# Delta rule stage: order of PE, ACT, DVE and POOL work around the block inverse changed

## The reference

```python
mixed = lax.conv_general_dilated(mixed, conv_w, (1,), [(3, 0)], ...)   # q, k, v: depthwise, 4 taps
g = -jnp.exp(A_log) * jax.nn.softplus(a + dt_bias)
beta = jax.nn.sigmoid(b)
q = _l2norm(q) * DK ** (-0.5)
k = _l2norm(k)
def step(Sstate, xs):
    q_t, k_t, v_t, g_t, b_t = xs
    Sstate = Sstate * jnp.exp(g_t)[..., None, None]
    kv = jnp.einsum('bhk,bhkv->bhv', k_t, Sstate)
    delta = (v_t - kv) * b_t[..., None]
    Sstate = Sstate + k_t[..., :, None] * delta[..., None, :]
    o_t = jnp.einsum('bhk,bhkv->bhv', q_t, Sstate)
    return (Sstate, o_t)
...
o = o * lax.rsqrt(var + EPS) * norm_weight * jax.nn.sigmoid(z)
return o.reshape(Bsz, Sl, VDIM) @ w_out.T
```

## Time and profile before

| | |
|---|---|
| median of 3 runs | 4793.93 us |
| the profiled execution | 4783.35 us, its span 4781.6 us |
| mean granted TensorE clock over the span | 0.881 |
| PE busy | 4103.1 us, 86% of the span |
| DVE busy | 2333.8 us, 49% |
| ACT busy | 1674.0 us, 35% |
| POOL busy | 1300.2 us, 27% |

### The profile page before, as it was taken

The page is one execution under the profiler, slowest core; times in us unless marked ns, Lnnn a source line. Parts: engine busy times, 40 slices in busy tenths (PEclk is TensorE's granted clock), DMA queues, the critical chain, the costliest instruction groups (busy, mean ns, idle before and its releaser), DMA issues. The chain is left out here.

```text
span 4781.6 us, 104546 instructions
## 1 busy us (share of the span) xinstructions
PE 4103.1 (86%) x45120; PEld 2471.8 (52%) x45120; DVE 2333.8 (49%) x4105; ACT 1674.0 (35%) x2632; POOL 1300.2 (27%) x1755
## 2 busy tenths in 40 slices
PE   7789759999965867778899779999999999999869
PEld 3333645555542733445645546655555665556546
DVE  5942244444453233342132256666666666666541
ACT  2057222112120102323111145555555555655432
POOL 2000110000015051220000045555554555555412
PEclk9689759999986985888899879998999999989879
DMA  1000000000020520000100000000000000000000
GB/s 46 1 1 2 28 25 1 10 10 1 10 95 27 172 78 17 0 0 23 54 0 0 5 10 8 9 9 9 9 9 8 10 8 8 8 8 8 6 14 18
DMA packets 37963, 91.85 MB, mean 19 GB/s; under 512 B 6992, under 2 KB 27251, under 8 KB 33998
## 3 DMA queue, kind: packets, MB, share of 16 engines
q1 hardware_dynamic: 27150, 69.45, 4.3%
q0 software_dynamic: 6144, 11.62, 0.8%
q10 hardware_dynamic: 4224, 4.19, 0.3%
HBM read 69.96 MB, written 20.45 MB: 19 GB/s over the span
## 5 line engine op out<-in xcount | busy, mean ns | idle before, releaser
L2498 PE MATMUL ps<-h_normT,h_w 128*128 128x512 f32 (+1 forms) x1008 | 446.0, 549 | 69.8 <-DVE h_xx L3086 62.7
L3020 DVE SCALAR_TENSOR_TENSOR h_cv<-h_raw,h_cw,h_cv 128x1023 f32<-128x1023 f32 (+2 forms) x288 | 385.4, 1339 | 19.8 <-ACT h_cv L2847 18.8
L3164 DVE SCALAR_TENSOR_TENSOR h_st<-h_st,d_gcs,ps 128x64 f32<-128x64 f32 x448 | 122.7, 274 | 402.6 <-PE ps L2795 402.4
L2395 POOL TENSOR_TENSOR h_gm<-h_gm,h_tmp 128x15 f32<-128x15 f32 (+7 forms) x480 | 268.7, 560 | 37.6
L2846 ACT ACTIVATE h_raw<-ps 128x512 f32<-128x512 f32 x192 | 114.1, 594 | 460.0 <-PE ps L2498 459.2
L2498 PEld LDWEIGHTS ps<-h_normT,h_w 128*128 128x128 f32 x1008 | 173.0, 199 | 175.1 <-issue 157.6
L837 PE MATMUL ps<-a_probT,a_v 128*128 128x512 f32 x512 | 227.8, 604 | 0.9 <-DVE a_probT L975 0.9
L1960 PE MATMUL ps<-h_normT,e_wgu 128*128 128x512 f32 (+1 forms) x448 | 203.8, 598 | 3.3 <-DMA e_wd<-in_e_wd 2.7
L2394 POOL TENSOR_TENSOR h_tmp<-h_gm 128x15 f32<-128x15 f32 (+7 forms) x480 | 185.1, 386 | 64.4 <-DVE h_gm L3073 29.3
L1124 POOL MEMSET r_zero<- 128x2048 f32 x1 | 1.8, 1804 | 727.2 <-POOLq L54 727.2
L2795 PEld LDWEIGHTS ps<-h_st,h_mT 64*64 64x64 f32 x1792 | 91.7, 135 | 199.9 <-issue 194.8
(11 more groups left out here) (537 smaller groups left out, 9513.9 us busy)
## 6 DMA issues: line engine op xcount, KB each, us to landing
m_wgu<-in_m_wgu SPq DMA_DIRECT2D x8, 1408.0 KB
h_w<-in_d_w SPq DMA_DIRECT2D x48, 128.0 KB
m_wd<-in_m_wd SPq DMA_DIRECT2D x8, 704.0 KB
m_rows_in<-r_zero SPq DMA_DIRECT2D x4, 1024.0 KB
e_xe<-m_rows_in SPq DMA_DIRECT2D x8, 512.0 KB
m_rows_out<-e_y ACTq DMA_DIRECT2D x8, 512.0 KB
e_wgu<-in_e_wgu SPq DMA_DIRECT2D x1, 3520.0 KB
a_t_raw<-in_t_w SPq DMA_DIRECT2D x4, 768.0 KB
```

Source lines behind the costliest of these rows:

```text
L2395: c.link(pool.tensor_tensor(target, target, part, ALU.subtract))
L2498: last = pe.matmul(ps[:, PROJ[m], lo:hi], w[:, kind, k, :], hT[:, k, b * S + tb * BANK + lo:b * S + tb * BANK + hi], start=(k == 0), stop= ...
L3020: dve.scalar_tensor_tensor(out=d, in0=raw[:, kind, 0:S - back], scalar=tap(pr, kind, TAPS3 - 1 - back), in1=d, op0=ALU.mult, op1=ALU.add). ...
```

## The change

On PE the second key products and the decay sums up to each token go ahead of the second value product. In `states`, the third output product goes from c = 10 to c = 9, and from the first bank of A3 to B3 + 1; the inverse then starts at c = 10; the quarters of projections 4 and 5 are spread over c = 10 to 13, two of projection 4 standing alone at c = 11; the two halves of the last output product stand behind `inverse_below` and `inverse_above`, at c = 14 and 15. On POOL the gating goes first in the step. On ACT both output copies go first, the output squares behind and between the key squares and decays; it compacts two quarters instead of three, ahead of the second value parts. DVE compacts the third quarter, does the transposes and the gathering ahead of the query sums, and has its convolutions, residual sums and copies of the inverse at other q.

```diff
@@ heads3
-        POUT = (B3 + 1, B3 + 1, A3, A3)
+        POUT = (B3 + 1, B3 + 1, B3 + 1, A3)
@@ gpsimd: sided(f)
                 pool.wait_ge(sub, SUBS * (f[0] + 1))
+                if f[0]:
+                    pool.wait_ge(wk, 2 * f[0])
@@ gpsimd: step
+                if t:
+                    gated(t)
                 if f:
                     scaled(f)
                 if t:
                     squares(t)
                 if f:
                     last_quarter(f, t)
-                if t:
-                    gated(t)
-                if f:
                     solve(f)
                     sided(f)
@@ tensor: key_side
                     key_products(f, 0)
+                if f:
+                    hold(k_ev, 3 * f[0] + 3)
+                    key_products(f, 1)
+                    pe.wait_ge(at_d, 2 * f[0] + 1)
+                    decay_upto(f)
                 if t:
                     hold(sqo_d, 2 * n)
                 values_and_keys(1)
-                if f:
-                    hold(k_ev, 3 * f[0] + 3)
-                    key_products(f, 1)
                 key_sums(0)
                 key_sums(1)
-                if f:
-                    pe.wait_ge(at_d, 2 * f[0] + 1)
-                    decay_upto(f)
@@ tensor: states, beside(c)
-                    if c == 9 and f:
+                    if c == 9 and t:
+                        pe.wait_ge(xa, 4 * n + 2)
+                        project_out(t, 2)
+                    if c == 10 and f:
                         if p:
-                            pe.wait_ge(xa, 4 * n + 2) if t else pe.wait_ge(ev, 6 * p[0] + 2)
+                            pe.wait_ge(xa, 4 * n + 3) if t else pe.wait_ge(ev, 6 * p[0] + 2)
                         hold(zv, 2 * n + 2)
-                        inverse_y(f, (lambda k: project(p, 4, k)) if p else None)
-                    if c == 10 and t:
-                        pe.wait_ge(v_ev, f[0] + 1) if f else pe.wait_ge(lnd, 2 * t[0] + 2)
-                        project_out(t, 2)
-                    if c == 11 and f:
+                        inverse_y(f, (lambda k: project(p, 4, k) if k < 2 else None) if p else None)
+                    if c == 11 and p:
+                        for k in (2, 3):
+                            project(p, 4, k)
+                    if c == 12 and f:
                         hold(v_ev, f[0] + 1)
-                        hold(ev, 6 * p[0] + 5) if p else hold(xa, 4 * n + 2)
-                        inverse_z(f, (lambda k: project(p, 5, k)) if p else None)
-                    if c == 12:
-                        if t:
-                            pe.wait_ge(xa, 4 * n + 3)
-                        if f:
-                            inverse_zt(f, (lambda k: out_part(t, 3, 0) if k == 0 else None) if t else None)
-                        elif t:
-                            out_part(t, 3, 0)
-                    if c == 13:
+                        hold(ev, 6 * p[0] + 5) if p else hold(xa, 4 * n + 3)
+                        inverse_z(f, (lambda k: project(p, 5, k) if k < 3 else None) if p else None)
+                    if c == 13 and f:
+                        inverse_zt(f, (lambda k: project(p, 5, 3) if k == 0 else None) if p else None)
+                    if c == 14:
                         if f:
                             inverse_below(f)
                         if t:
+                            pe.wait_ge(v_ev, f[0] + 1) if f else pe.wait_ge(lnd, 2 * t[0] + 2)
+                            out_part(t, 3, 0)
+                    if c == 15:
+                        if f:
+                            inverse_above(f)
+                        if t:
                             out_part(t, 3, 1)
-                    if c == 14 and f:
-                        inverse_above(f)
@@ scalar: step
                 if t:
-                    outputs(t, 0)
+                    outputs(t)
                 if f:
-                    key_squares(f)
+                    key_squares(f, (0,))
                 if t:
-                    outputs(t, 1)
+                    output_squares(t, 0)
                 if f:
+                    key_squares(f, (1,))
                     decays(f)
+                if t:
+                    output_squares(t, 1)
                 parts(0)
+                if f:
+                    compacted(f)
                 parts(1)
...
-                    if f and g == 1:
-                        compacted(f)
@@ scalar: outputs
+            def outputs(t):
+                if t[0]:
+                    act.wait_ge(y_p, 4 * t[0])
+                for a in range(2):
+                    act.wait_ge(o_p, NC3 * t[0] + NC3)
+                    act.activation(chunks(o[:], a), outs(a), ACT.Copy).then_inc(o_d, 1)
+            def output_squares(t, a):
+                act.wait_ge(o_p, NC3 * t[0] + NC3)
+                act.activation(chunks(sqo, a), outs(a), ACT.Square).then_inc(sqo_d, 1)
@@ vector
+            def third_quarter(f):
+                dve.wait_ge(nt_d, 2 * f[0] + 2)
+                dve.tensor_copy(y[quarter(2), :, :], nT[quarter(2), :, side(2)]).then_inc(nc2_d, 1)
@@ vector: step
                     decayed(f, 0)
                     decayed_pairs(f, 0)
-                    convolve(f, 6)
                     decayed(f, 1)
                     decayed_pairs(f, 1)
+                    third_quarter(f)
+                    diagonals(f)
+                    gather(f)
                 for g in range(2):
...
-                if f:
-                    diagonals(f)
-                    gather(f)
...
-                    if f and q in (1, 2):
-                        convolve(f, q + 6)
+                    if f and q in (1, 2, 3):
+                        convolve(f, q + 5)
...
-                    if t and q == 6:
-                        add(t, 0)
-                    if t and q == 8:
-                        add(t, 1)
+                    if t and q in (6, 8, 10):
+                        add(t, (q - 6) // 2)
...
-                    if f and q == 10:
+                    if f and q == 11:
                         masked(f)
-                    if t and q == 11:
-                        add(t, 2)
-                    if f and q in (12, 13):
-                        refined(f, q - 12)
+                    if f and q in (13, 14):
+                        refined(f, q - 13)
...
-                    if p and q in (3, 5, 6, 9, 10, 12):
-                        convolve(p, (3, 5, 6, 9, 10, 12).index(q))
+                    if p and q in (5, 6, 7, 10, 11, 12):
+                        convolve(p, (5, 6, 7, 10, 11, 12).index(q))
```

More of the change, by code:

```diff
@@ L2262, in heads3 @@
                  "sqvr", "bepd", "kev", "vev", "seg", "decd", "dbd", "egp", "egx", "qed", "qsqd", "kk", "ntd", "atd",
-                 "ncd", "nc3d", "xtd", "nqd", "ndd", "sub", "xmd", "xdd", "nx", "yd", "y4d", "xy", "xd", "tt", "xtx", "uwp", "wd", "ud", "wk", "mtd", "ptd",
+                 "ncd", "nc2d", "nc3d", "xtd", "nqd", "ndd", "sub", "xmd", "xdd", "nx", "yd", "y4d", "xy", "xd", "tt", "xtx", "uwp", "wd", "ud", "wk", "mtd", "ptd",
                  "sp", "sd", "loc", "op", "od", "sqod", "sqa", "msp", "lnd", "rsd", "rz", "ond", "yp", "xa")
@@ L2266, in heads3 @@
          sqv_r, bep_d, k_ev, v_ev, seg, dec_d, db_d, eg_p, egx, qe_d, qsq_d, kk, nt_d, at_d,
-         nc_d, nc3_d, xt_d, nq_d, nd_d, sub, xm_d, xd_d, nx, y_d, y4_d, xy, x_d, tt, xtx, uw_p, w_d, u_d, wk, mt_d, pt_d,
+         nc_d, nc2_d, nc3_d, xt_d, nq_d, nd_d, sub, xm_d, xd_d, nx, y_d, y4_d, xy, x_d, tt, xtx, uw_p, w_d, u_d, wk, mt_d, pt_d,
          s_p, s_d, loc, o_p, o_d, sqo_d, sqa, ms_p, lnd, rs_d, rz, on_d, y_p, xa) = (ph.sem(n) for n in names)
@@ L2817, in end @@
                 for k in range(4):
-                    if k in (1, 3):
+                    if k in (1, 2):
                         pe.wait_ge(xa, 4 * n + 4 + k)
-                    if k == 2:
+                    if k == 3:
                         pe.wait_ge(lnd, 2 * n + 2)
@@ L2852, in gate_logits, with key_squares @@
                 act.activation(zs[:, b, half(tb)], ps[:, GATE[tb], :], ACT.Sigmoid).then_inc(zv, 1)
-            def key_squares(f):
+            def key_squares(f, some=range(2)):
                 n = f[0]
-                for a in range(2):
+                for a in some:
                     act.wait_ge(k_ev, 3 * n + 1) if a else act.wait_ge(trk, n + 1)
@@ L2892, in compacted @@
                 act.wait_ge(nt_d, 2 * n + 2)
-                for r in range(3):
+                for r in range(2):
                     act.activation(y[quarter(r), :, :], nT[quarter(r), :, side(r)], ACT.Copy).then_inc(nc_d, 1)
@@ L2988, in step @@
                     inverse_pieces(f)
-            def outputs(t, a):
-                n = t[0]
-                chunks = lambda v, a: v.rearrange("p (j a n) -> p a j n", a=2, n=CH3)[:, a]
-                act.wait_ge(o_p, NC3 * n + NC3)
-                src = ps[:, C3 + a, :].rearrange("p (j n) -> p j n", n=CH3)
```

(17 more changed lines are left out.)

## The result

The changed kernel takes 4932.24 us, the median of 4 runs (4904.42 to 4944.69), against 4793.53 (4789.97 to 4810.0) for the kernel before: ratio 1.0279, 95% interval 1.0252 to 1.0307. It is 2.8% slower. The forecast was 4790 with a range up to 4850: no change was expected, and the time lies 82 us above the range.

What follows compares the result with a forecast made beforehand. The prediction took PE, 86% busy, as the bound, with waits and low clock at the inverse's head and tail. Queues +1.1 and clock -1.2 gave -0.1 per unit, x29 = -3 us: 4790 us, range 4715 to 4850.

Steps and rivals of the forecast that it cites:

- POOL: POOL's substitution before the block inverse: 2.8 us earlier against PE, so POOL leaves the path.
- Head: Head of the block inverse: new stalls of 1.05 (state) and 1.5 us (residual sum) on DVE; net +0.45 per unit.
- Middle: Before chunk 12: PE waits for ACT to copy the fifth projection's bank, +0.9 us per unit.
- Tail: Last small products of the inverse: the 1.09 us wait for DVE's 32-row copy goes, -1.1 per unit.
- Key side: Key products and sums: waits for scaled keys 0.4, decayed pairs 0.1, ACT's copies 0.55; +1.05 per unit, 0.2 hidden.
- Clock: PE's granted clock: -1.5 at the tail, +0.3 at the head, net -1.2 us per unit; about 0.94 over the stage.
- POOL and DVE beside each other: Convolution beside POOL's substitution: each costs the other 0.5 to 0.7 us; taken as hidden, else some +5 us in all.
- B: Rival, chance 0.28: the bank handover puts DVE's queue on PE's path at chunk 10; +1.6 per unit, 4840 us.
- A: Rival, chance 0.23: the clock holds at the tail of the inverse; -1.5 per unit, 4750 us.
- C: Rival, chance 0.11: handovers hide, both PE waits and most low clock go; -3.6 per unit, 4690 us.

Runs made afterwards that it cites:

- e2: The kernel before with only the changed chunk loop and the wait it needs; POOL, ACT and key side in the old order: 4865.87 us, ratio 1.0145.
- e4: The changed kernel with the first three of p's convolutions one state update earlier, at q = 4, 5, 6: 4858.78 us, ratio 1.0122.
- e3: The changed kernel with the second value product again ahead of the second key products, and ACT's two compacted quarters behind its second value parts: 4877.97 us.
- e10: The changed kernel with the third output product back in bank A3, at c = 11, its sum at q = 12; inverse still from c = 10: 4813.57 us.
- e9: The changed kernel with the old key side of the second value product, convolutions at q = 4, 5, 6, 10, 11, 12 and values at q = 11: 4737.72 us.

## Why the prediction was wrong

Per unit it had +1.1 at full clock and -1.2 from the clock; measured are +4.05 and +0.6. The miss is 4.7 us per unit, 2.9 in the queues and 1.8 in the clock. Two steps failed: the head, by its size, and the clock, which had nothing for the stall before chunk 12.

*POOL*: right. It leaves the path, with 7.2 us between its first sided product and the transposes.

*Head*: this step failed by its size. The mechanism, the place and the last two stalls were right (0.88 and 1.53 against 1.05 and 1.5). It began the count at the convolution of q = 7 and took 1.2 for it, with PE and DVE in step until then. They were not: the convolution at q = 5 takes 2.06 and that at q = 7 1.87, and PE waits at the chunks before too. State waits are 2.1 instead of 1.05: 0.85 before chunk 10 and 1.25 before chunks 7 to 9. The prediction took the 1.2 from rows where POOL was not beside it. e2, with the convolutions at the same q, POOL late and each at 1.27 to 1.30, has no wait before chunks 7 to 9, and e4, with them earlier, has next to none.

*Middle*: right, 1.2 for 0.9. *Tail*: the wait is gone as counted, 1.1.

*Key side*: 0.7 for scaled keys and pairs and 0.4 for the value parts, 1.1 where 1.05 was counted; the 0.2 said to be hidden were not. e3 gives back 1.6 per unit, more than the waits.

*Not counted*: gaps for which the trace shows no releaser rose by 0.6 per unit. Half of that is the missing matmul record of each unit; so the true rise is about 0.3, before the 32-row products, and the rest rose by about 0.9. What makes these two is open.

*Clock*: this step failed in its sign, -1.2 against +0.6. The head was right: 24 units fall instead of 15, for 2.15 instead of 1.90 lost, +0.25 where +0.3 was counted. What the table calls tail is two places. In 14 units the clock falls at the tail proper, for 1.6 us per unit instead of 2.65: -1.1 where -1.5 was counted, with falls in half of the units. In 5 units it falls at 30.4 to 31.5 us, 1.3 us behind the new stall on ACT's copy, mostly for 17.1 us at a stretch: 1.4 per unit, counted at nothing. In e10, where that stall is 0.3 instead of 1.2, no unit falls there; but e10 also has an output product at that place, and in e9 the stall stays and no unit falls behind it. So the stall is where these falls stood, and not shown to be enough for one.

The 14 at the tail proper fall though the wait for DVE's copy is gone. PE still stood still ahead of each, for 0.45 to 1.7 us in the last 6, nearly all of it in gaps without a releaser; the stretch 3069 to 3075 above is such a case. The term took one wait as the cause where others stand near it.

*POOL and DVE beside each other*: the prediction weighed this for POOL's sake and found it hidden. It came out at another place: beside POOL's wide products it is DVE that is late, and DVE is on the path at the head. The Trainium skill (SBUF — State Buffer, SBUF: two separate sides, on the shared port pair) has VectorE, in an operation with two SBUF inputs, and GpSimd hold one pair of ports by an exclusive lock: whichever starts first keeps it for its whole instruction. The trace agrees in both directions: 2.06 instead of 1.27 for a convolution that starts behind POOL's product, and 1.90 and 2.02 instead of 1.04 for the gate products that start behind a convolution. The prediction's price for a square was too high: it took 1.04 as its length alone, but away from the convolution the squares take 1.27 in the changed kernel. No run kept the change's order and moved POOL's gate products alone, so what the meeting costs by itself is not measured.

*Rivals*: B named the right place and the right direction, and its sign of the clock held (0.91, under its 0.92). Its price, 1.6 per unit, was a third of the measured one, since it used the same durations as the forecast. The handover, with the later place of its product and sum, is worth 70 of the 139 us by e10, the convolutions 77, the key side 57, and these overlap. A fell: the wait went and the clock did not hold. C fell: new stalls took the place of the old ones.

## What to carry to other kernels

When work moves to another place in a queue, take its duration from beside what will run there, not from where it ran: here 1.27 became 2.06 and 1.87, two of three in a row, on the engine that had just become the last. A PSUM bank that is handed on just ahead of the critical product puts the reader's whole queue on the path; here it was better to put the product that frees it behind, where it covers another wait. An engine made early gains only if nothing else is late at the same place, so change the chunk loop and the early work one at a time: one gave 25 us, both together cost 139. A new stall may bring the clock down behind it as well as hold the engine up: give it a term in both sums.

## What was not expected of the hardware

With a wait of 1.1 us behind them, two added full-width products brought the falls of TensorE's clock from 22 to 10 of 27 units, and 32 added 32-row products raised them to 26, most of them ahead of that wait. So the wait was neither enough for a fall nor needed for one. Taking a wait away from a place full of 32-row products did not keep the clock up either: in the changed kernel it still fell there in 14 of 27 units, behind gaps of 0.45 to 1.7 us for which the trace shows no releaser.

VectorE and GpSimd slowed each other by turns: a VectorE operation of 1.27 us took 2.06 when a GpSimd product was running at its start, and the GpSimd product behind it took 1.90 instead of 1.04.
